# Fourth block: first rows and first weights prepared one stage ahead, in buffers that three stages share

## What is computed

```python
# third block's MLP:  x = x + gelu(rmsnorm(..) @ mlp_w1 + mlp_b1) @ mlp_w2 + mlp_b2
# fourth block
x1 = layer_norm(x, ln1_w, ln1_b)
q = (x1 @ q_w + q_b);  k = ctx @ k_w + k_b;  v = ctx @ v_w + v_b      # 16 heads of 32
out = softmax(q k^T / sqrt(32), masked) v @ cproj_w + cproj_b
hidden = out + x
y = gelu(layer_norm(hidden, ln2_w, ln2_b) @ fc_w + fc_b)               # 512 -> 2048
return hidden + y @ proj_w + proj_b
```

## Time and profile before

| | us |
|---|---|
| median of 3 runs (2777.37 to 2783.21) | 2779.68 |
| the profiled execution | 2779.15 |
| its span, first to last instruction | 2777.1 |
| PE busy in the span | 2638.4 (95%) |
| DVE, ACT, POOL busy | 1450.3, 782.8, 392.3 |
| mean granted clock of TensorE | 0.983 of full speed |

### The profile page before, as it was taken

How to read it: one execution, slowest core, us unless ns; L and a number is a source line. 1 busy time by engine, 2 the same in 40 slices (tenths; PEclk the granted TensorE clock), 3 DMA queues, 4 the chain that set the end, 5 groups by cost and what they waited for, 6 DMA issues and landing times. The chain is left out here.

```text
span 2777.1 us, 30412 instructions
## 1 busy us (share of the span) xinstructions
PE 2638.4 (95%) x12328; PEld 1928.4 (69%) x12328; DVE 1450.3 (52%) x2282; ACT 782.8 (28%) x1363; POOL 392.3 (14%) x282
## 2 busy tenths in 40 slices
PE   9999999999899999989999999979999889799999
PEld 7777778777678888745454444358888656578887
DVE  6466566655764443445445454375343586763443
ACT  4322332233231111215335353431011244321110
POOL 0000000000130000014334243441000310220000
PEclk9999999999899999999999999999999999999999
DMA  4100110110100000222212122120000100100001
GB/s 192 51 35 36 61 61 16 46 61 1 50 16 31 31 0 1 104 77 56 53 40 59 54 49 49 40 110 31 16 16 1 69 1 0 65 13 19 31 1 61
DMA packets 35604, 118.28 MB, mean 43 GB/s; under 512 B 8069, under 2 KB 8198, under 8 KB 25994
## 3 DMA queue, kind: packets, MB, share of 16 engines
q1 hardware_dynamic: 35466, 116.35, 12.7%
HBM read 81.18 MB, written 7.34 MB: 32 GB/s over the span
## 5 line engine op out<-in xcount | busy, mean ns | idle before, releaser
L1607 DVE TENSOR_REDUCE l_top<-l_slot 128x1 f32<-128x512 f32 x256 | 170.8, 680 | 204.2 <-PE l_slot L1409 203.6
L1558 ACT ACTIVATE l_weighed<-l_across 128x512 f32<-128x512 f32 (+1 forms) x320 | 183.7, 595 | 291.0 <-PE l_across L1433 287.6
L389 PE MATMUL l_wide<-l_key_map,l_norm 128*128 128x260 f32 x1024 | 235.2, 383 | 2.7 <-ACT l_norm L544 2.3
L389 PEld LDWEIGHTS l_wide<-l_key_map,l_norm 128*128 128x128 f32 x1024 | 191.7, 190 | 32.1 <-ACT l_norm L544 2.7
L1433 PE MATMUL l_across<-l_q_stack,l_k_stack 99*128 99x512 f32 (+1 forms) x320 | 192.2, 604 | 10.9 <-ACT l_weighed L1558 7.8
L1236 POOL TENSOR_TENSOR l_paired<-l_weighed 128x2048 f32<-128x2048 f32 x32 | 145.6, 4549 | 379.3 <-ACT l_weighed L1558 323.7
L725 DVE TENSOR_TENSOR x<-l_added,x 128x512 f32<-128x512 f32 x128 | 87.1, 688 | 82.0 <-PE l_added L131 60.5
L1433 PEld LDWEIGHTS l_across<-l_q_stack,l_k_stack 99*128 99x128 f32 (+1 forms) x320 | 57.6, 181 | 97.0 <-issue 65.6
L1409 PE MATMUL l_slot<-l_k_stack,l_q_stack 97*128 97x512 f32 x256 | 111.3, 435 | 11.1 <-DMA l_k_stack<-l_k_parts 6.5
L2405 ACT ACTIVATE l3m_hidden<-l3m_up,columns 128x512 f32<-128x512 f32 x64 | 44.2, 692 | 271.1 <-PE l3m_up L131 259.0
L2405 ACT ACTIVATE l2m_hidden<-l2m_up,columns 128x512 f32<-128x512 f32 x64 | 44.2, 693 | 270.4 <-PE l2m_up L131 265.6
(11 more groups left out here) (391 smaller groups left out, 5952.6 us busy)
## 6 DMA issues: line engine op xcount, KB each, us to landing
l_k_stack<-l_k_parts SPq DMA_DIRECT2D x192, 72.0 KB, 2.0
l_q_stack<-l_q_parts SPq DMA_DIRECT2D x192, 64.0 KB, 2.0
l_wk<-in_weights SPq DMA_DIRECT2D x9, 1024.0 KB, 4.8
l_wv<-in_weights SPq DMA_DIRECT2D x9, 1024.0 KB, 4.9
l_wo<-in_weights SPq DMA_DIRECT2D x9, 1024.0 KB, 4.8
l_wqT<-in_weights SPq DMA_DIRECT2D x8, 1024.0 KB, 6.9
l0m_raw<-in_weights SPq DMA_DIRECT2D x8, 1024.0 KB, 4.8
l2m_raw<-in_weights SPq DMA_DIRECT2D x8, 1024.0 KB, 4.9
```

The source lines that it names most:

```text
L389: last = pe.matmul(wide[:, j, 0:W], norm[:, k, at:at + P], key_map[:, k, b, :, :].rearrange("p h c -> p (h c)"), start=k == 0, stop=k == K ...
L1558: act.activation(weighed[0:height(c), (CHUNKS * g + c) % RING, j, :], across[0:height(c), use % 2, :], ACT.Exp)\
L1607: dve.tensor_reduce(top[:, t, j:j + 1], slot[:, i % 2, :], AX.X, ALU.max, negate=True).then_inc(s["top_ready"], 1)
```

## The change

A class `Handover` holds buffers that live from the third block's MLP to the end: the two raw weight buffers (which are also the attention's `queries`), the high and low weights (the attention's `wq_hi` and `wq_lo`, the MLPs' `w1h` and `w1l`), the rows, and statistics of one batch. The three stages run within one function.

- The third block's MLP computes, in its last round, the moments of batch 0 (`next_moments`, DVE, ahead of the additions of the third chunk), its root (ACT, after the last activation) and its rows (`next_rows`, DVE, before the last four additions).
- The attention starts without `moments(0)`, `roots(0)` and `scale_rows(0)`: PE transposes at once. Its SP queue loads `wk` ahead of `wq`; ACT takes all four norm tiles before it casts `wq`; DVE's order of lows, keys and mask changes; POOL adds the bias of batch 0 without waiting for rows.
- Within the attention, SP loads the first block of fc1 when batch 2's logits are done, POOL splits it when the last query product is done (8 instructions), DVE computes batch 0's moments after `normalise(2, 3)` and its rows after `shift(3, 0)`, and ACT its root.
- The last MLP starts with rows and first weights ready (`prepared`): no first load of `raw1`, no split of it, no first moments, root and rows; the load of fc1's second block is issued at once.

```diff
+class Handover:
+
+
+    def __init__(self, n, rows, mem):
+        self.rows = rows
+        self.raw = n.sbuf("handover_raw", [P, 2, KT, D], F32, mem)
+        self.high, self.low = (n.sbuf(f"handover_{w}", [P, KT, D], F32R, mem) for w in ("high", "low"))
+        self.stats = n.sbuf("handover_stats", [P, TPB, 6], F32, mem)
+        self.mean_var = n.sbuf("handover_mean_var", [P, TPB, 2], F32, mem)
+        self.second, self.deviation, self.spread = (n.sbuf(f"handover_{w}", [P, TPB], F32, mem) for w in ("second", "deviation", "spread"))
+
+    def moments(self, n, dve, link, ready):
+        for j in range(TPB):
+            link(dve.bn_stats(self.stats[:, j, :], n.x[:, j, :]), j == TPB - 1)
+        for j in range(TPB):
+            link(dve.bn_aggr(self.mean_var[:, j, :], self.stats[:, j, :]), j == TPB - 1)
+        dve.tensor_scalar(self.second[:, :], self.mean_var[:, :, 1], 1e-5, None, ALU.add).then_inc(ready, 1)
+
+    def scale_rows(self, n, dve, link):
+        link(dve.reciprocal(self.spread[:, :], self.deviation[:, :]))
+        for j in range(TPB):
+            dve.tensor_scalar(self.rows[:, j, :], n.x[:, j, :], self.mean_var[:, j, 0:1], self.spread[:, j:j + 1], ALU.subtract, ALU.mult)
 
 
 def product3(pe, out, left, right, start, stop):
...
+            sp.dma_start(wk, n.block("l3_wk")).then_inc(s["wk_loaded"], 16)
             sp.dma_start(wq_raw, n.block("l3_wq")).then_inc(s["wq_loaded"], 16)
-            sp.dma_start(wk, n.block("l3_wk")).then_inc(s["wk_loaded"], 16)
...
+            sp.wait_ge(s["logits_done"], (B - 1) * TPB)
+            sp.dma_start(shared.raw[:, 0, :, :], n.block("l3_fc1", 0)).then_inc(s["next_loaded"], 16)
+            sp.wait_ge(s["next_loaded"], 16)
...
-                pool.wait_ge(s["rows_ready"], b + 1)
+                if b:
+                    pool.wait_ge(s["rows_ready"], b)
...
+            pool.wait_ge(s["next_loaded"], 16)
+            pool.wait_ge(s["work_done"], WORK["query", B - 1, GROUPS - 1] + 1)
+            for k in range(KT):
+                pool.tensor_copy(shared.high[:, k, :], shared.raw[:, 0, k, :]).then_inc(s["next_high"], 1)
+                pool.wait_ge(s["next_high"], k + 1)
+                pool.tensor_tensor(shared.low[:, k, :], shared.raw[:, 0, k, :], shared.high[:, k, :].bitcast(F32), ALU.subtract)
...
-                if k == 0:
-                    pe.wait_ge(s["rows_ready"], b + 1)
+                if b and k == 0:
+                    pe.wait_ge(s["rows_ready"], b)
...
-            roots(0)
+            def next_roots():
+                act.wait_ge(s["next_variance"], 1)
+                act.activation(shared.deviation[:, :], shared.second[:, :], ACT.Sqrt).then_inc(s["next_deviation"], 1)
+
+            for k in range(KT):
+                take_norm(0, k)
             act.wait_ge(s["wq_loaded"], 16)
             for k in range(KT):
                 act.copy(wq_hi[:, k, :], wq_raw[:, k, :]).then_inc(s["wq_high"], 1)
-            for k in range(KT):
-                take_norm(0, k)
...
+                if b == B - 2:
+                    next_roots()
...
-            moments(0)
-            scale_rows(0)
-            take_mask()
...
+            def next_moments():
+                for t in range(TPB):
+                    use = ("out", 0, t)
+                    dve.wait_ge(work_free[WORK[use] % 2], work_uses(use))
+                shared.moments(n, dve, link, s["next_variance"])
+
+            def next_rows():
+                dve.wait_ge(s["next_deviation"], 1)
+                dve.wait_ge(s["turned_done"], TURNED["norm", B - 1, KT - 1] + 1)
+                shared.scale_rows(n, dve, link)
+
             lows(0, 0)
+            lows(0, 1)
             take_keys(0)
-            lows(0, 1)
             lows(0, 2)
             take_keys(1)
             lows(0, 3)
             take_keys(2)
             take_keys(3)
+            take_mask()
...
+                if not more:
+                    next_rows()
...
+                if b == B - 2:
+                    next_moments()
...
-        raw2 = n.sbuf(f"{tag}_raw2", [P, KT, D], F32, mem)
+        if shared is not None:
+            raw1, raw2, w1h, w1l = shared.raw[:, 0, :, :], shared.raw[:, 1, :, :], shared.high, shared.low
...
-            sp.dma_start(raw1[:, :, :], n.block(first, 0)).then_inc(raw1_loaded, 16)
+            if not prepared:
+                sp.dma_start(raw1[:, :, :], n.block(first, 0)).then_inc(raw1_loaded, 16)
...
-                sp.wait_ge(w1_ready, splits(f - 1))
+                if w1_splits(f - 1):
+                    sp.wait_ge(w1_ready, w1_splits(f - 1))
...
+            if not prepared:
+                pool.wait_ge(raw1_loaded, 16)
+            for k in range(0 if prepared else KT):
...
-                pe.wait_ge(rows_ready, c + 1)
+                if c >= FIRST:
+                    pe.wait_ge(rows_ready, c + 1 - FIRST)
...
-                            if c == 0:
+                            if c == 0 and not prepared:
                                 pe.wait_ge(w1_ready, k + 1)
...
-            roots(0)
+            if not prepared:
+                roots(0)
...
+            if shared is not None and not prepared:
+                act.wait_ge(variance_ready, B + 1)
+                act.activation(shared.deviation[:, :], shared.second[:, :], ACT.Sqrt).then_inc(deviation_ready, 1)
...
+            if not prepared:
+                moments(0)
+                scale_rows(0)
...
+                    if shared is not None and not prepared and f == FB - 1 and c == B - 2:
+                        next_moments()
                     add_downs(f, c)
+                    if shared is not None and not prepared and f == FB - 1 and c == B - 2:
+                        next_rows()
...
+        shared = Handover(n, rows, mem)
...
+                  kind="rms", eps=1e-6, src_dram=n.dram["l2_rows"], kept=rows, shared=shared)
+        n.end_stage()
+        l3_attention(n, shared)
+        n.end_stage()
+        mlp_stage(n, "l3m", "l3m_scale", "l3m_offset", "l3_b2", "l3_fc1", "l3_fc2", "l3_b1", ACT.Gelu_apprx_tanh,
+                  kept=rows, out_dram=n.dram["out"].rearrange("(t p) d -> p t d", p=P), shared=shared, prepared=True)
```

More of the change, by code:

```diff
@@ L1708, in l3_attention @@
     with ExitStack() as mem:
-        wq_hi, wq_lo, wo_hi, wo_lo = (n.sbuf(f"l3_{w}", [P, KT, D], F32R, mem) for w in ("wq_hi", "wq_lo", "wo_hi", "wo_lo"))
+        wq_hi, wq_lo, queries, rows = shared.high, shared.low, shared.raw, shared.rows
+        wo_hi, wo_lo = (n.sbuf(f"l3_{w}", [P, KT, D], F32R, mem) for w in ("wo_hi", "wo_lo"))
         norm_hi, norm_lo = (n.sbuf(f"l3_norm_{w}", [P, KT, S], F32R, mem) for w in ("hi", "lo"))
         mixed_hi, mixed_lo = (n.sbuf(f"l3_mixed_{w}", [P, GROUPS, S], F32R, mem) for w in ("hi", "lo"))
-        queries = n.sbuf("l3_queries", [P, 2, GROUPS, S], F32, mem)
         keys = n.sbuf("l3_keys", [P, GROUPS, B, 4, C], F32, mem)
@@ L1716, in l3_attention @@
         probs_T = n.sbuf("l3_probs_T", [P, PAIRS, S], F32, mem)
-        rows = n.sbuf("l3_rows", [P, TPB, D], F32, mem)
         bv_row = n.sbuf("l3_bv_row", [P, D], F32, mem)
@@ L2071, in scale_rows @@
             def scale_rows(b):
-                dve.wait_ge(s["deviation_ready"], b + 1)
+                dve.wait_ge(s["deviation_ready"], b)
                 link(dve.reciprocal(spread[:, b, :], deviation[:, b, :]))
-                if b:
-                    dve.wait_ge(s["turned_done"], TURNED["norm", b - 1, KT - 1] + 1)
+                dve.wait_ge(s["turned_done"], TURNED["norm", b - 1, KT - 1] + 1)
                 for j in range(TPB):
@@ L2221, in _, with mlp_stage @@
             add_out(B - 1, 3)
-def mlp_stage(n, tag, scale, offset, row, first, second, bias, activation, kind="layer", eps=1e-5, src_dram=None, kept=None, out_dram=None):
+def mlp_stage(n, tag, scale, offset, row, first, second, bias, activation, kind="layer", eps=1e-5, src_dram=None, kept=None, out_dram=None, shared=None, prepared=False):
     nc = n.nc
@@ L2257, in element, with w1_splits @@
             return (c + B - 1) % B if src_dram is not None else c
+        FIRST = 1 if prepared else 0
         def splits(f):
             return KT + f
+        def w1_splits(f):
+            return f if prepared else splits(f)
         def turned_bank(c, k):
@@ L2302, in _ @@
         def _(pool):
-            pool.wait_ge(raw1_loaded, 16)
-            for k in range(KT):
+            if not prepared:
+                pool.wait_ge(raw1_loaded, 16)
+            for k in range(0 if prepared else KT):
                 pool.tensor_copy(w1h[:, k, :], raw1[:, k, :]).then_inc(w1_high, 1)
@@ L2332, in ups @@
                     if m == 0 and c == 0 and f:
-                        pe.wait_ge(w1_ready, splits(f))
+                        pe.wait_ge(w1_ready, w1_splits(f))
                     if f or c:
@@ L2473, in split_w1 @@
             def split_w1(f):
[L2474 removed]
+                dve.wait_ge(raw1_loaded, 16 * (f + 1 - FIRST))
```

(22 more changed lines are left out.)

20 lines of the change are left out of this document (10 added, 10 removed).

## The result

| | kernel before | the change |
|---|---|---|
| median, us | 2776.7 (15 runs) | 2781.45 (15 runs, 2776.05 to 2787.46) |
| ratio | | 1.0016, interval 1.0008 to 1.0023 |
| the profiled execution, its span | 2779.15, 2777.1 | 2776.05, 2774.3 |
| its mean granted clock | 0.983 | 0.990 |
| at the same clock (below) | 0 | +7.5 +- 0.9 us |

The account below looks back on a forecast made before the run. PE, busy 95% of the span, was taken as the bound, with time only in its waits at two heads. Terms 0 + 1.5 + 0 - 4.9 = -3.4 from 2779.15 gave 2775.7, plus 0.5 for the median: 2776.2 us, range 2770.5 to 2781.5.

Parts of the forecast that it names:

- time is to be had only where PE waits or runs at the lower clock: Opening step, whole kernel: PE works 95% of the span, so only its waits or lower clock offer time.
- 0 + 1.5 + 0 - 4.9: Sum over third block's MLP tail, attention's start, between the batches and last MLP's head: -3.4 us.
- The attention's start, +1.5: Start of the fourth attention: late casts put POOL's additions on DVE's batch 1 scalings; +1.5 us, bounds -2.8 and +3.6.
- the forecast's middle: Attention's start: +1.5 us, between +0.7 if PE's clock rises during the first key product and +2.6 if not.
- Between the batches and the third block's tail, 0: Two terms: added moments, scalings, roots and table loads there fall into idle time or cover; 0 us each.
- The last MLP's head, -4.9: Last MLP's start: PE transposes earlier, DVE's scalings start at 2409.9 against 2414.82; -4.9 us, bounds -6.2 and -3.5.
- the gain arrives whole: Last MLP: every link behind the scalings hangs on the one before, so all 4.9 us reach the end.
- Its own sign of being wrong: Last MLP: the prediction is wrong if start to end is shortened by less than 3.5 us.
- slower: Starvation rival, attention and last MLP: DVE's scalings wait for POOL's whole series; +2.2 us together, 2781.9 us, chance 0.08.
- slower by more: Whole kernel slower by more than 5.6 us, needing a starvation wait in the third place too; chance 0.04.
- The bound given, 0.2%: Whole kernel: a measurement tells about 0.2% (5.6 us) from no change; chance 0.64 of staying within it.

Follow-up runs that it names:

- e1: The change plus one unused tensor of 32 bytes per partition behind the handover's small tensors; ratio 0.9993 to the kernel before, -0.8 us at the same clock.
- e4: e1 with the attention's start put back to the code of before, last MLP still prepared; ratio 0.9983 to the kernel before, -3.2 us at the same clock.
- e5: e1 with the mask's transfer queued ahead of wq's and the mask built ahead of the first keys; ratio 0.9966 to the kernel before.
- e7: e1 with both the early mask of e5 and the late bias additions of e6; ratio 0.9975 to the kernel before, median 2770.5 us.
- e6: e1 with POOL's bias additions of batch 0 put behind the scalings of batch 1; ratio 0.9964 to the kernel before, -4.7 us at the same clock.

## Why the prediction was wrong

**The missed term.** The step that failed is the first one: "time is to be had only where PE waits or runs at the lower clock". It takes for granted that PE's own matmuls cost what they cost before; the sum, 0 + 1.5 + 0 - 4.9, has no term for them, and no reason is given for putting it at nothing. The change allocates its shared buffers so that the weights lie 32 bytes off the norm tiles modulo 256, and that made the 1536 ups 6 ns longer: +9 us by count and stretch, +8.2 +- 1.2 by e1 against the change (which holds the query products too). The instruction orders of the two kernels are the same there, and no row of before hints at it except the 398 ns of `l_added` beside the 389 of the downs, which were not compared.

**The attention's start, +1.5.** Measured +2.4 +- 1.2 (with the third block's tail), inside the bounds. The chain to POOL's additions held within 0.6 us at each link (2201.05, 2201.74, 2216.22); ACT's last read came at 2216.25 for 2215.3, 0.2 of it from the slower query products. The place of the contention did not hold. I let the scalings of batch 1 start at 2216.4 and take 5.4; they started at 2220.08 and took 2.73. DVE was not free earlier: the change puts the mask behind the keys, where it took 2.77 beside POOL's last `wq_lo` and its clearing of `values` instead of 0.55, and the three L2108 operations took about 1.0 each beside the `wo` split and the additions, two of which took 0.17 before. I had costed the mask's move at nothing and had let the contention fall on one place; it fell on four, the mask, two more of L2108 and the scalings. That `shift(0, 0)` still came at 2222.85, where the forecast's middle gives 2222.6, is luck.

**Between the batches and the third block's tail, 0.** For the work between the batches e4 agrees: it has the old start and the new work there, and 211.9 us to the last matmul, the mean of the kernels with the old attention. The tail has no kernel of its own; the attention's first instructions start 1.6 us behind the last product of the third block's MLP in both traces (2187.30 behind 2185.72 before, 2187.30 behind 2185.68 after).

**The last MLP's head, -4.9.** e4 gives -3.2 +- 0.9 at the same clock; the stretch to the first `l3m_down` is 46.0 us on average in the six kernels with the old head and 40.1 to 43.8, mean 41.9, in those with the new one, so -4.1. Mechanism and place right, size somewhat too large. The scalings started even earlier than forecast (2408.96 against 2409.9); on average the gain didn't arrive whole at the first down, though the prediction said "the gain arrives whole". Its own sign of being wrong was met here: from its start to the end the MLP went from 375.3 us to 373.2, 2.1 shorter where at least 3.5 was asked, because the slower ups took back 4.5.

**Sum.** +2.4 - 3.2 = -0.8 without the missed term, against -3.4 forecast; +7.5 with it. (That this is e1 is no test, as the +2.4 is the difference of e1 and e4.) All of this is at the same clock. The median of the change, 2781.45, lies just inside the stated range of 2770.5 to 2781.5, but only because the forecast started from a median 3 us too high; the direction was wrong. Of the rivals, "slower" had the right sign for a wrong reason: DVE was not starved, the scalings never waited for a whole POOL series. Its chance (0.08, of which 0.04 was "slower by more") came from a list of waits alone; a cause of another kind, a change of every instruction's price, was not on the list. The bound given, 0.2%, would call the outcome no change; with fifteen runs a side the interval lies above 1.

## What to carry to other kernels

When a change adds, shares or moves buffers, compare the mean duration of the same matmuls before and after, and the addresses of their two operands: a small tensor allocated between big ones cost each of 1536 matmuls here 6 ns, and putting the big tensors at multiples of 256 bytes took nothing but the bytes. A head that is prepared early is worth only what the engine behind the next wait can use; here POOL's clearing, split and additions, made later by the new order, ran beside DVE's mask, moments and scalings and took the gain. And compare kernels at the same granted clock where executions differ in it, with the plain medians beside it.

## What the runs showed of the hardware

- A 128x512 product of these kernels has a median duration of 389 ns (226.4 ns from one to the next) with loaded and moving operand at addresses that agree modulo 256 bytes per partition, and of 393 to 396 (about 233) where the loaded operand lies 32, 64 or 128 bytes past the moving one. Shown for split (float32r) operands: weights against norm tiles, hidden tiles against weights, and `l_added`, whose median went from 394 to 389 ns. Two kinds of plain float32 products did not change (384 and 604 ns).
- The time of one kernel follows the mean granted clock by 16.7 us per 0.01, and 1.6 us of scatter (standard deviation) is left of the 12 us between executions; the rest goes with the clock.
- An operation of DVE on a 128x4 tile, 0.17 us alone, took 0.86 to 1.03 beside POOL's `wo` split and additions in the change; the 128x256 mask took 0.29 alone (e5, e7) and 2.30 to 2.77 beside the end of POOL's `wq_lo` and its clearing of `values` (e6, e1, the change). Four 128x512 scalings took 1.92 us alone, 2.73 over the last POOL addition and 4.63 over the last three.
